# Full attention: the value groups of neighbouring key tiles put together in the step's order

## What is computed

```
qh = proj(q, W_q, b_q); kh = proj(k, W_k, b_k); vh = proj(v, W_v, b_v)
scores = einsum('bhqd,bhkd->bhqk', qh, kh) / sqrt(16)
scores = where(mask == 0, -1e9, scores)
attn = softmax(scores, axis=-1)
context = einsum('bhqk,bhkd->bhqd', attn, vh)
```

## Time and profile before

| | |
|---|---|
| median of three runs | 5008.25 us (5003.82 to 5016.03) |
| profiled execution | 5015.41 us, of which span 5013.7 us |
| TensorE busy in the span | 4695.7 us, 94%, mean granted clock 0.95 |
| DVE busy | 3711.5 us, 74% |
| ACT busy | 2785.7 us, 56% |
| DVE's maxima of items (L1163) | 2027.0 us in 3392 instructions |
| ACT's exponentials (L1139) | 1745.9 us in 3328 |
| value matmuls (L1245) | 886.3 us in 6656 |

### The profile page before, as it was taken

One profiled execution on the slowest core, in us unless ns is written; L12 is line 12 of the kernel. 1 busy time (PEld: TensorE's weight loads), 2 busy tenths in 40 slices (PEclk: granted clock), 3 DMA queues, 4 the chain that ended last, 5 costly groups with the idle time before them and its releaser, 6 DMA issues. The chain is left out here.

```text
span 5013.7 us, 93794 instructions
## 1 busy us (share of the span) xinstructions
PE 4695.7 (94%) x28527; PEld 2782.3 (55%) x28528; DVE 3711.5 (74%) x8768; ACT 2785.7 (56%) x5123; POOL 1283.7 (26%) x936
## 2 busy tenths in 40 slices
PE   8979997998579999999999999999999767999998
PEld 4546655777244444444444444444443556988897
DVE  7768875663858888888888888888886576555654
ACT  2325552222327777777778777778777113444443
POOL 5630001221721011101011011011010222666665
PEclk9989998999779999999999999999998777999999
DMA  6657754221872333433333433423321551333332
GB/s 179 175 144 191 188 160 121 83 77 51 266 166 45 70 65 72 81 72 58 68 64 73 81 68 54 76 62 75 67 51 19 155 169 30 64 79 68 65 65 37
DMA packets 298233, 470.40 MB, mean 94 GB/s; under 512 B 57304, under 2 KB 216056, under 8 KB 297712
## 3 DMA queue, kind: packets, MB, share of 16 engines
q1 hardware_dynamic: 268224, 426.93, 35.4%
q0 software_dynamic: 26144, 36.26, 4.5%
q10 hardware_dynamic: 3360, 0.98, 0.1%
HBM read 238.55 MB, written 144.94 MB: 76 GB/s over the span
## 5 line engine op out<-in xcount | busy, mean ns | idle before, releaser
L1163 DVE TENSOR_REDUCE full_peak<-full_item 128x1 f32<-128x512 f32 (+2 forms) x3392 | 2027.0, 655 | 352.8 <-PE full_item L1225 336.8
L1139 ACT ACTIVATE full_prob<-full_score 128x512 f32<-128x512 f32 (+1 forms) x3328 | 1745.9, 602 | 415.5 <-PE full_score L1235 396.9
L1225 PE MATMUL full_item<-full_kst,full_qst 49*128 49x512 f32 (+1 forms) x4096 | 1176.4, 405 | 8.4 <-DMA full_kst<-full_high 5.5
L1235 PE MATMUL full_score<-full_qst,full_kst 51*128 51x512 f32 (+1 forms) x3328 | 1033.5, 436 | 7.4 <-issue 6.7
L1225 PEld LDWEIGHTS full_item<-full_kst,full_qst 49*128 49x128 f32 x4096 | 621.5, 189 | 604.7 <-DVE full_peak L1163 536.7
L1245 PE MATMUL full_value<-full_prob,full_vaug 128*17 128x512 f32 x6656 | 886.3, 605 | 0.9 <-ACT full_raw L1127 0.5
L1235 PEld LDWEIGHTS full_score<-full_qst,full_kst 51*128 51x128 f32 (+1 forms) x3328 | 508.3, 183 | 375.0 <-ACT full_prob L1139 297.2
L1078 POOL TENSOR_TENSOR full_low<-full_low,full_keep 128x1601 f32<-128x1601 f32 x32 | 115.9, 3622 | 2017.6 <-ACT full_low L1113 2017.6
L2421 ACT ACTIVATE moe_h<-moe_hbank,moe_b 128x384 f32<-128x384 f32 (+1 forms) x320 | 199.8, 624 | 442.6 <-PE moe_hbank L2592 402.9
L2602 PE MATMUL moe_ybank<-moe_w_both,moe_h_high 128*128 128x512 f32 x1088 | 386.7, 396 | 0.0
L2455 DVE TENSOR_TENSOR moe_h_low<-moe_h,moe_h_high 128x384 fp32r<-128x384 f32 (+1 forms) x320 | 194.3, 618 | 221.9 <-ACT moe_h_high L2411 221.8
(11 more groups left out here) (283 smaller groups left out, 6856.7 us busy)
## 6 DMA issues: line engine op xcount, KB each, us to landing
full_kst<-full_high SPq DMA_DIRECT2D x256, 200.1 KB
full_ctxT<-in_ctxT SPq DMA_DIRECT2D x16, 1601.0 KB, 8.2
full_kst<-full_low SPq DMA_DIRECT2D x128, 200.1 KB
win_qst<-scratch_q SPq DMA_DIRECT2D x384, 64.0 KB, 2.8
full_qst<-scratch_q SPq DMA_DIRECT2D x384, 64.0 KB
scratch_attn<-win_raw SPq DMA_DIRECT2D x64, 256.0 KB
scratch_q<-open_parts SPq DMA_DIRECT2D x64, 256.0 KB, 3.7
scratch_attn<-full_raw SPq DMA_DIRECT2D x64, 256.0 KB, 2.2
```

Of the source, the lines that this page charges most:

```text
L1139: nc.scalar.activation(prob_of(s, h, kt)[0:rows, :], score[score_bank(u)][0:rows, :], ACT.Exp, scale=SCALE).then_inc(score_read, 1)
L1163: nc.vector.tensor_reduce(peak[s.par][:, hq:hq + len(qts), c], src, AX, ALU.max).then_inc(item_read, 1)
L1225: ins = nc.tensor.matmul(ps[:, at:at + z - a], qst[s.slot][rows, h // 2, qt * P:(qt + 1) * P].bitcast(F32R), kst[s.slot][rows, h // 2, a:z ...
L1235: nc.tensor.matmul(score[score_bank(u)][0:z - a, :], kst[s.slot][rows, h // 2, a:z].bitcast(F32R), qst[s.slot][rows, h // 2, :].bitcast(F3 ...
```

## The change

`STEP_ORDER` gets another string; no other line changes. There are 13 Vs in it as before. The first stays alone. The other twelve now stand as six pairs, `VV`: key tiles 0 and 1, 2 and 3, 4 and 5, 6 and 7, 8 and 9, 10 and 11, each pair where the second of the two stood. The sequence of S, I and J is the same.

```
@@ -845,8 +845,8 @@
-    STEP_ORDER = ("SSISIVISSIISJSIISISJISISSIVISISSISVSSIIIJIISSISVSISISISVIISSISVSIISSSIIIVISIISVISSIIVSISISIVISSISIJI"
-                  "SISSISIVISISSIVSIISSIVI")
+    STEP_ORDER = ("SSISIVISSIISJSIISISJISISSIISISSISVVSSIIIJIISSISSISISISVVIISSISSIISSSIIIVVISIISISSIIVVSISISIISSISIJIS"
+                  "ISSISIVVISISSISIISSIVVI")
```

## The result

The changed kernel takes 5413.83 us (median of 4 runs, 5412.02 to 5431.94) where the kernel before, run beside it, takes 5006.7: a ratio of 1.082 [1.0805, 1.0834]. It is slower by 407 us, where the prediction said 272 and drew its range to 5400.

The account below looks back on a forecast made before the run. TensorE sets the pace, with DVE within 0.1 us of bounding too. 5008 us plus 269 (4.34 a step over 62 steps) plus some 3 for clock falls gave 5280 us; own range 5215 to 5350, wider range 5215 to 5400.

Parts of the forecast that it names:

- The wait for three item banks: Six items in a row wait for DVE to empty three banks: 4.75 us instead of 3.76, +4.34 us a step.
- The gain of a double group: Two value groups together save tiling-mode changes on TensorE: 0.28 us a pair, 1.7 a step, 108 us.
- rival A: Faster: the saved ways in and out of value groups decide, DVE's wait stays hidden; 4900 us, chance 0.03.
- The probability buffers at nothing: ACT's wait for value groups to free probability buffers lies beside DVE's wait: costed at nothing, at most 63 us.
- ACT's score banks behind DVE: ACT's chain through four score banks takes 3.96 us for six scores, under DVE's 4.75.
- a few falls of the clock: TensorE's granted clock falls in single steps only: some 3 us in all.
- rival B: Much slower: rows of six items make the granted clock fall, 4 us a step on top; about 5530 us, chance 0.11.
- What would show it: Right: steps some 4.3 us longer, last items 0.60 apart, mean value matmul unchanged. Wrong: granted clock below 0.95, among others.

Follow-up runs that it names:

- e3: The changed kernel with DVE's maxima taken over only the first half of each item's columns: 5166.55 us, 1.0315 of the kernel before.
- e11: The changed kernel with full matmuls, but maxima over the first 64 columns and exponentials of the first 64 queries only: 4887.87 us, 0.9758 of the kernel before.
- e12: The kernel before with maxima over the first 64 columns and exponentials of the first 64 queries only: 4962.03 us, 0.9906 of the kernel before.
- e5: The changed kernel with half of each maximum and half of each exponential left out: 4992.22 us, 0.9965 of the kernel before.
- e7: The changed kernel with 15 overwritten matmuls a step added in the item rows ahead of tiles 4 to 9: 5332.45 us, 1.0647 of the kernel before.
- e1: The changed kernel with only the pairs of key tiles 0-1, 2-3 and 10-11 put together: 5161.87 us, 1.0306 of the kernel before.
- e2: The changed kernel with only the pairs of key tiles 4-5, 6-7 and 8-9 put together: 5226.7 us, 1.0435 of the kernel before.

## Why the prediction was right, and where it failed

- **The wait for three item banks** was right in place, mechanism and size: 4.74 from double group to double group for 4.75, and 4.43 us a step at full clock for 4.34. Pair by pair at full clock: +0.75 to 0.85, +0.72 to 0.83, +0.76, +0.51, +0.78, +0.80, for the predicted +0.76, +0.75, +0.76, +0.51, +0.75, +0.81. e3 shows that it is DVE: with half maxima the step at full clock gets back 2.12 of the 4.43, until ACT is next. No run changed the number of banks; that it is three which bind is read from the fourth item's wait and its length.
- **The gain of a double group** was real and hidden, as forecast: rival A lacked only short round trips. e11 against e12 has 1.2 us a step for the predicted 1.7. The Trainium skill, TensorEngine Tiling (Array Packing), section Key Properties, says that changing the tiling mode drains TensorE; e11 agrees, with 0.11 to 0.32 us for each pair of changes saved.
- **The probability buffers at nothing**: held. The wait that the prediction named is there, once a step (ACT waits for a value group 23 times in the 1000 us, 6.7 us in all), and the pairs cost what DVE's pace alone gives. ACT's score banks behind DVE, at 3.96 against 4.75, were rightly named as covered; e3 and e5 show how soon they are next.
- **The clock** is the step that failed: "a few falls of the clock (rival B in single steps) are worth some 3 us". It was some 120 us. Rival B's mechanism came in two thirds of the steps, beside the forecast's and not in place of it, at about 7.62 - 4.43 = 3.2 us a step where B had 4 in every step. The argument against B was that the rows "are broken by 1.9 us of dense value matmuls"; the clock fell between dense double groups all the same, and the groups then took 3.5 us instead of 1.91. The range made room for B in a third of the steps, and the result lies 14 us above it. With 120 in place of 3 the prediction's sum is 5277 + 120 = 5397, 17 us under the result; the jobless steps, whose +23 us had been counted as two steps of 4.34, are 14 of that. By e7 the clock's part is nearer 107, and then 13 us more stay open.
- **What would show it** was well chosen: "a granted clock in the stretch below 0.95, which would add B" is what the profile shows, with 0.94; and the mean of a value matmul, which was to stay, rose from 598 to 662 ns.

The price of B was at hand: the first step without jobs in the earlier trace rows has a row of nine items at DVE's pace, and a clock of 0.79. What the prediction did not do was to give the forecast more than 3 us of B; otherwise it made them exclude each other. The Trainium skill, TensorE: Matmul & The Clock Gate, section A second HAM failure mode: psum-queue depth-cycling, tells of idle moments between matmul groups at which the clock swings; the trace agrees here with 362 us at the lower level, and e7 with 99 us once more matmuls stand in these rows.

What stays open: why the rows ahead of tiles 4 to 9 lose the clock and those ahead of 0 to 3 and 10 to 11, which the wait makes longer by as much, do not. What these runs show is that the place in the step matters (e1 and e2) and that more work on TensorE in these rows keeps the clock (e7). One difference is in the trace: in the step of 40.36 us TensorE stood idle, by its rows, for 0.82 of the 17.1 us of tiles 4 to 9 and for 0.30 of the 16.6 us of tiles 0 to 3. No run sets this apart from the place.

## What to carry to other kernels

A producer's row between two long groups that holds more pieces than the consumer has banks is to be counted by the round trip of one bank, and not by the two engines' paces alone. Here three banks carried rows of three and cost 0.51 to 0.85 us in rows of six or eight, and rows of six cost nothing once the round trips of DVE and ACT were short (e11). Where a change makes TensorE wait often and briefly, price the granted clock as a part of the forecast, from the nearest stretch of the trace that waits like that, and not only as a rival to it.

## What the runs showed of the hardware that was not expected

Additional matmuls made a kernel faster by 81 us (5413.83 to 5332.45): what they cost, the granted clock gave back and more. And the falls of the clock were not additive: 235 us at the lower level with the inner pairs alone, 51 with the outer alone, 362 with both, where the kernel before has 61.
